# An adaLN transformer block on one core: score operands gathered by 16 transfers per half batch in place of 24, v by two per batch

## The reference

```python
x = L0_attn_x                              # 8 x 512 x 256, f32
mod = (silu(L0_c) @ L0_wmod).reshape(8, 6, 1, 256)
sa, ca, ga, sb, cb, gb = (mod[:, i] for i in range(6))   # gates ga, gb: |.| at least 0.25
h = layernorm(x) * (1 + ca) + sa
x = x + ga * attn_block(h)                 # LN, 16 heads of 16, band of 128 keys, softmax,
                                           # out-projection, LN, 256 -> 1024 -> 256 with gelu
h = layernorm(x) * (1 + cb) + sb
return x + gb * channel_mix(h)             # mixes each row with the one before; sigmoid(r) * (relu(k)^2 @ Wv)
```

## Time and profile before

| | |
|---|---|
| time, median of 3 runs | 644.75 us (642.35 to 646.23) |
| the profiled execution's own time | 644.62 us |
| its span, first to last instruction | 642.9 us |
| PE busy | 579.4 us (90%) |
| PE weight loads | 454.9 us (71%) |
| ACT busy | 449.8 us (70%) |
| DVE busy | 418.7 us (65%) |
| POOL busy | 384.1 us (60%) |
| transfers | 63516 packets, 55.74 MB, mean 87 GB/s |

### The profile page before, as it was taken

How to read it: one execution, slowest core, us unless ns; L and a number is a source line. 1 busy time by engine, 2 the same in 40 slices (tenths; PEclk the granted TensorE clock), 3 DMA queues, 4 the chain that set the end, 5 groups by cost and what they waited for, 6 DMA issues and landing times.

```text
span 642.9 us, 16628 instructions
## 1 busy us (share of the span) xinstructions
PE 579.4 (90%) x6494; PEld 454.9 (71%) x6494; DVE 418.7 (65%) x847; ACT 449.8 (70%) x758; POOL 384.1 (60%) x610
## 2 busy tenths in 40 slices
PE   5888888799889999989998999999899989999986
PEld 2667575669667777767766777677667768877775
DVE  4775584647676668667876868576857485365543
ACT  2533634588687978698869877887879788955542
POOL 3400874637775765857776767765777369835321
PEclk9978988799989999999999999999999999999999
DMA  7534321323441222433253414341333131311110
GB/s 239 194 92 128 84 58 52 86 68 102 112 115 53 79 57 69 124 91 104 57 136 83 112 44 112 108 114 47 94 97 95 51 97 44 93 36 34 34 42 33
DMA packets 63516, 55.74 MB, mean 87 GB/s; under 512 B 14459, under 2 KB 52669, under 8 KB 63438
## 3 DMA queue, kind: packets, MB, share of 16 engines
q1 hardware_dynamic: 60454, 52.64, 29.1%
q10 hardware_dynamic: 2984, 2.05, 1.2%
HBM read 22.31 MB, written 4.49 MB: 42 GB/s over the span
## 4 chain that ended last, share of the span: by engine, by line
PE 52%; DVE 16%; ACT 14%; SPq 5%; POOL 5%; issue 4%; DMA 3%; ACTq 0%; DVEq 0%; POOLq 0%
PE bank L351 4%; DVE nmax L1519 4%; PE bank L468 4%; PE quad L330 3%; PE bank L456 3%; PE bank L480 3%; PE bank L429 3%; PE bank L430 3%; PE bank L431 3%; PE quad L380 3%; PE bank L229 3%; ACT bank L1021 3%; SPq L2536 2%; SPq L2538 2%; PE quad L257 2%
## 5 line engine op out<-in xcount | busy, mean ns | idle before, releaser
L970 ACT ACTIVATE p<-quad,scale_s 128x768 f32<-128x768 f32 (+1 forms) x90 | 73.3, 825 | 17.4 <-PE quad L330 16.0
L2151 POOL TENSOR_SCALAR_AFFINE_SELECT p<-p 128x448 f32<-128x448 f32 x64 | 40.3, 630 | 73.9 <-ACT p L975 45.6
L1519 DVE TENSOR_REDUCE nmax<-quad 128x8 f32<-128x1032 f32 x64 | 78.9, 1233 | 2.2
L1021 ACT ACTIVATE bank<-bank,bias,scale_g 128x256 f32<-128x256 f32 x128 | 63.1, 532 | 17.3 <-PE bank L414 17.1
L412 PE MATMUL bank<-bt_hi,w_hi 128*128 128x256 f16 x256 | 70.3, 275 | 4.1 <-DVE hid_lo L1579 4.0
L429 PE MATMUL bank<-w_hi,hid_hi 128*128 128x256 f16 x256 | 69.9, 273 | 1.4 <-DVE hid_lo L1579 0.9
L413 PE MATMUL bank<-bt_lo,w_hi 128*128 128x256 f16 x256 | 69.9, 273 | 0.0
L414 PE MATMUL bank<-bt_hi,w_lo 128*128 128x256 f16 x256 | 69.8, 273 | 0.0
L431 PE MATMUL bank<-w_hi,hid_lo 128*128 128x256 f16 x256 | 69.8, 273 | 0.0
L430 PE MATMUL bank<-w_lo,hid_hi 128*128 128x256 f16 x256 | 69.8, 273 | 0.0
L2166 POOL TENSOR_TENSOR ps<-p 128x384 f32<-128x384 f32 x64 | 65.2, 1019 | 3.1 <-PE quad L363 1.3
(11 more groups left out here) (226 smaller groups left out, 1509.1 us busy)
## 6 DMA issues: line engine op xcount, KB each, us to landing
v_blk<-vn SPq DMA_DIRECT2D x64, 128.0 KB, 2.6
k_st<-kt_hi SPq DMA_DIRECT2D x120, 64.0 KB, 2.0
rb<-den_rows SPq DMA_DIRECT2D x16, 256.0 KB
x<-x SPq DMA_DIRECT2D x16, 256.0 KB, 3.1
out<-x SPq DMA_DIRECT2D x16, 256.0 KB, 2.3
q_st<-qt_hi SPq DMA_DIRECT2D x120, 32.0 KB, 1.9
k_st<-kt_lo SPq DMA_DIRECT2D x60, 64.0 KB, 2.0
xa<-x SPq DMA_DIRECT2D x7, 512.0 KB, 5.0
```

The source lines that it names most:

```text
L970: e.activation(p32[gp % SLOTS][:, c0:c0 + 2 * w].rearrange("p (n c) -> p n c", n=2), quad[:, b0:b0 + 2, 0:w], ACT.Exp, scale=scale_s[:, 1: ...
L1021: e.activation(dst, dst, ACT.Gelu_apprx_tanh, bias=bias_1[:, m:m + 1], scale=scale_g[:, 0:1]).then_inc(s_gl, 1)
L1519: e.tensor_reduce(nmax[:, :, :, qt].rearrange("p a j -> p j a"), quad[:, :, 2 * QB - 2:2 * WIN].rearrange("p j (c a) -> p j a c", a=2), AX ...
```

## The change

The high and low parts of q become two planes of one tile `q_two`, those of k two planes of `k_two`; the old names are views of them. One transfer then writes 64 rows of `q_st`, each row's high and low part after one another, and one writes 64 rows of `k_st` with each row of `kt_hi` twice. The third 32 rows are gathered as before. Four transfers per group take the place of six. `vn` and `v_blk` get another order of dimensions, so that two transfers of 512 KB, in pieces of 4 KB, move the v of a whole batch, where eight of 128 KB did. There is one `load_v(n)`, in the place of `load_v(n, 0)`; it waits for `s_av` of 2n, both contexts of the batch before. The rest of each engine's order is kept. The core of the diff:

```diff
-        qt_hi, qt_lo = sb("qt_hi", [P, L], F16), sb("qt_lo", [P, L], F16)
-        kt_hi, kt_lo = sb("kt_hi", [P, 2 * L], F16), sb("kt_lo", [P, 2 * L], F16)
+        q_two, k_two = sb("q_two", [P, 2, L], F16), sb("k_two", [P, 2, 2 * L], F16)
+        qt_hi, qt_lo, kt_hi, kt_lo = q_two[:, 0, :], q_two[:, 1, :], k_two[:, 0, :], k_two[:, 1, :]
...
-        vn = sb("vn", [P, NT, 2, 2, 2 * VW])
-        v_blk = sb("v_blk", [P, 2, 8, 2 * VW])
+        vn = sb("vn", [P, 2, NT, 2, 2 * VW])
+        v_blk = sb("v_blk", [P, 2, NT, 2, 2 * VW])
...
-                        e.wait_ge(s_stk[j], 6 * DMA * (u + 1))
+                        e.wait_ge(s_stk[j], 4 * DMA * (u + 1))
...
-                e.wait_ge(s_vin[half], 4 * DMA * (u // 2 + 1))
+                e.wait_ge(s_vin, 2 * DMA * (u // 2 + 1))
...
-                    for r, part in enumerate((qt_hi, qt_lo, qt_hi)):
-                        e.dma_start(q_st[2 * HD * r:2 * HD * (r + 1), half, j, :], part[src, :]).then_inc(s_stk[j], DMA)
-                    for r, part in enumerate((kt_hi, kt_hi, kt_lo)):
-                        e.dma_start(k_st[2 * HD * r:2 * HD * (r + 1), half, j, :], part[src, :]).then_inc(s_stk[j], DMA)
+                    e.dma_start(q_st[0:4 * HD, half, j, :], q_two[src, :, :]).then_inc(s_stk[j], DMA)
+                    e.dma_start(k_st[0:4 * HD, half, j, :], k_two[src, 0:1, :].broadcast_to([2 * HD, 2, 2 * L])).then_inc(s_stk[j], DMA)
+                    e.dma_start(q_st[4 * HD:SR, half, j, :], qt_hi[src, :]).then_inc(s_stk[j], DMA)
+                    e.dma_start(k_st[4 * HD:SR, half, j, :], kt_lo[src, :]).then_inc(s_stk[j], DMA)
...
-            def load_v(n, half):
+            def load_v(n):
...
                 e.wait_ge(s_v3, 4 * (n + 1))
-                hold(e, s_av, 2 * n - 1 + half if n else 0)
-                for a in range(2):
-                    for i in range(2):
-                        e.dma_start(v_blk[a:P:2, half, i:8:2, :], vn[KW * i:KW * (i + 1), :, a, half, :]).then_inc(s_vin[half], DMA)
+                hold(e, s_av, 2 * n)
+                for i in range(2):
+                    e.dma_start(v_blk[:, i, :, :, :], vn[KW * i:KW * (i + 1), :, :, :, :]).then_inc(s_vin, DMA)
...
             spread_den(0)
-            load_v(1, 0)
+            load_v(1)
             fold_den(1)
...
             save_den(2)
-            load_v(1, 1)
             spread_den(2)
             stacks(4, 0, 4)
             load_residual(0)
-            load_v(2, 0)
+            load_v(2)
             rows_gates()
...
             spread_den(3)
-            load_v(2, 1)
             load_mod_a(4)
```

More of the change, by code:

```diff
@@ L152, in adaln_block @@
         s_x, s_moda = sem("x_in"), sem("moda_in")
-        s_vin = [sem(f"v_in_{i}") for i in range(2)]
+        s_vin = sem("v_in")
         s_stk = [sem(f"stacks_{j}") for j in range(HQ)]
@@ L350, in context @@
                     for j in range(HQ):
-                        e.matmul(bank[32 * j:32 * j + 32, s * KW:s * KW + w], v_blk[:, half, s, 2 * j * HD:2 * (j + 1) * HD],
+                        e.matmul(bank[32 * j:32 * j + 32, s * KW:s * KW + w], v_blk[:, s % 2, s // 2, half, 2 * j * HD:2 * (j + 1) * HD],
                                  p32[(4 * u + j) % SLOTS][:, c:c + w], start=(s == 0), stop=(s == 7))
@@ L929, in high_qk @@
                 for j in range(HQ):
-                    hold(e, s_stk[j], 6 * DMA * u)
+                    hold(e, s_stk[j], 4 * DMA * u)
                 e.activation(qt_hi[:, :], ring_s.at["qk", u, 0][:, :], ACT.Identity, bias=bias_q[:, 2 * m:2 * m + 1]).then_inc(s_qh, 1)
@@ L943, in copy_v @@
                 e.wait_ge(s_v, 2 * n + t2 + 1)
-                hold(e, s_vin[0], 4 * DMA * n)
-                hold(e, s_vin[1], 4 * DMA * n)
-                rows = vn[:, 2 * t2:2 * t2 + 2, :, :, :].rearrange("p t a h (j b d) -> p t a (h j) b d", b=2, d=HD)
+                hold(e, s_vin, 2 * DMA * n)
+                rows = vn[:, :, 2 * t2:2 * t2 + 2, :, :].rearrange("p a t h (j b d) -> p a t (h j) b d", b=2, d=HD)
                 src = ring_s.at["v", n, t2][:, :].rearrange("p (t j b d) -> p t j b d", t=2, b=2, d=HD)
                 for a in range(2):
-                    e.activation(rows[:, :, a, :, a, :], src[:, :, :, a, :], ACT.Copy).then_inc(s_v3, 1)
+                    e.activation(rows[:, a, :, :, a, :], src[:, :, :, a, :], ACT.Copy).then_inc(s_v3, 1)
             def copy_den(u):
@@ L2645, in _ @@
             rows_bias()
-            load_v(0, 0)
-            load_v(0, 1)
+            load_v(0)
             stacks(1, 0, 2)
@@ L2693, in _ @@
                 store(u - 5)
-                load_v(b, 0)
+                load_v(b)
                 load_residual(u - 3)
-                load_v(b, 1)
                 fold_den(u)
@@ L2712, in _ @@
             store(7)
-            load_v(B - 2, 0)
+            load_v(B - 2)
             load_residual(9)
-            load_v(B - 2, 1)
             load_mod_o(4)
@@ L2725, in _ @@
             save_den(NU - 3)
-            load_v(B - 1, 0)
+            load_v(B - 1)
             spread_den(NU - 3)
@@ L2734, in _ @@
             load_mod_g(B - 2)
-            load_v(B - 1, 1)
             save_den(NU - 2)
```

## The result

The changed kernel took 656.88 us (median of 4 runs, 655.8 to 657.69) against 644.33 for the kernel before (median of 4, 642.35 to 646.23): a ratio of 1.0200, interval 1.0176 to 1.0224. It is slower, as forecast, by twice as much as forecast: 650.6 was predicted, with 654.6 as the upper end. The profiled execution took 655.8 us, span 654.1.

A forecast was written before the change was run, and what follows sets the result against it. PE was taken to bound the kernel (94% busy from 200 us), SP's 5% of the chain running beside it. Batch 1's +2.75 us, reduced to 2.25, grew to 6.0 with batch 2: 644.62 + 6.0 = 650.6 us, 8-in-10 range 645.8 to 654.6.

The forecast's parts named there:

- Gathers on SP: `stacks` gathers, 24 issues become 16 per half batch: 15.2 us become 10.1; 0 gained in the steady stage.
- Rival D: Larger transfers take proportionally longer to issue, 1.3 us more ahead of each `fold_den`: +2.6, 653.2 us; chance 0.04.
- Layouts, steady stage: Matmuls, ACT copies and weight loads keep counts and shapes: 0; from 200 us on PE is 94% full: 0.
- Gathers on ACT: Half batches 0 and 1, 12 issues become 8: 2.5 us less in ACT's queue, 0 gained.
- Batch 1: `load_v(1)` ahead of `fold_den(1)`: 1.05 MB takes 3.4 us, `rc` lands at 116.05 not 113.3, DVE and PE 2.75 late.
- What follows it: After batch 1, `stacks(4)` starts at 146.25 and lands by 160; ACT and PE waits go, shift falls to 2.25 us.
- Batch 2: `load_v(2)` ahead of `rows_gates`, `load_residual(1)` and `fold_den(3)`, which lands at 178.1; DVE and PE 6.0 us late in all.
- The sum: Whole kernel: profiled execution of 644.62 us plus 6.0 gives 650.6 us, 0.9% above.
- Rival A: At v's transfers, the small transfer passes the large ones, so only issue order costs: +2, 646.6 us; chance 0.15.
- Rival B: At `stacks(4)` and `high_qk(5)`, SP's chain gives time back if `rc(1)`, `rc(3)` are no later: 641.5 or 643 us; chance 0.13.
- Rival C: A 5 us stop at 174 may bring half-speed clock, 4 us losing 2, two stretches 3.5: 653 to 654 us; chance 0.10.

The follow-up runs named there:

- mv12: Changed kernel with `load_v(1)` moved behind `spread_den(1)` and `load_v(2)` behind `spread_den(3)`: 643.03 us, 0.9996 of the kernel before.
- two_q: Changed kernel with the second v transfer of batch 1 issued from ACT's queue, beside the first on SP: 657.26 us, ratio 1.0212 to before.
- stride: Changed kernel, each v transfer of batches 1 and 2 reading 64 source partitions two apart, not adjacent (wrong tokens): 650.50 us, ratio 1.0108 to before.
- small: Changed kernel, v transfers of batches 1 and 2 carrying a quarter of their bytes, same order and issues: 649.29 us, ratio 1.0071 to before.
- g_only: Kernel before with only the new gathers (16 transfers per half batch), v as before: 642.49 us, ratio 0.9972 to before.
- v_only: Changed kernel with the old gathers (24), so only v by two transfers is new: 656.02 us, ratio 1.0187 to before.

## Why the prediction was right in kind and wrong in size

*Gathers on SP:* right. 16 issues from 123.01 to 133.56, 10.55 us for the 10.1 forecast, at 0.57 to 0.61 each. Rival D fell with it: two issues of 512 KB took 1.24 us in front of `rc(1)`, no more than two of 128 KB. The 2.85 us of the two at 173.24 are not their size, as in `mv12` the same two took 1.25. One reading was off without changing the term: SP's wait for copied denominators, 96.0 us, is the largest of its waits but a third of their 280 us, not most. *Layouts, steady stage:* right, 0: from context 4 to the end 443.75 us for 443.6. *Gathers on ACT* lie ahead of context 1, where executions differ by more than they could cost: not shown.

*Batch 1:* right in mechanism, the size wrong, and this is the step that failed. The prediction gave 1.05 MB 3.4 us, at some 300 GB/s, and let `rc` land 0.45 us behind. In the slices of after, v's data run from 113.5 to about 118.5: 5.0 us, at 203 GB/s for the first half and faster after it. The rate was taken between the 128 KB transfers and `xa`, because the pieces were thought to matter; the source's partitions do, and by them the first were the nearest row. The bound of 4.4 us was too low as well: it took the engines for a fifth idle at 200 GB/s, and in `two_q` they were full at 203. Then `rc` is used at 120.47, 2 us behind the bulk of v and not 0.45. The slices show a thin tail after 118.5: small packets (under 512 B), `rc`'s for the most part, go out from 117.5 to 119.9 us, the last 18 of them from 119.7 on, right behind the last 4 KB packet of v. So `rc` landed when the latest DMA engine was through with v; why one was late no run tests. In `stride`, where the data stop short at 114.5, it is used at 115.03. Together PE's stop grew by 5.5 us, where 2.75 was forecast with 3.8 as the limit; the stretch grew by 4.65, mostly because PE was busy 0.75 us less in it (20.9 us for 21.6). That `rc` lies behind v, as the ring order has it, is plain: 6.6 us from its issue to its use, and 1.9 in `small`.

*What follows it:* right. `qt_hi` waits for `k_st` no more, and the stretch from context 2 to 3 is 0.85 us shorter; 0.5 was forecast. Either half of the change gives that alone: 29.9 us in `g_only` and in `v_only`.

*Batch 2:* the same error a second time. From the end of context 3 to `divide(3)` the prediction has 8.1 us (170.0 to 178.1), the trace 9.65 (173.13 to 182.78); before it was 4.35. `mod_rows` landed 6.9 us after that end and not 5.3: the rate again. So the stretch cost 5.6 in place of 3.75.

*The sum.* The spans differ by 11.2 us where 6.0 was forecast. Each place took 1.9 us more than its term, and the gain between them was 0.35 larger: 3.45 of the 5.2 us. 1.6 more lie ahead of context 1, where the two kernels differ in nothing that this account prices. The clock may be the cause: summed over windows of 2 us from 50 to 110, this execution had 16.2 us at the lower clock and that of before 13.6, and 2.6 us more at half speed would be some 1.3 us. That is not shown: `stride` had 17.1 us of it and context 1 at 110.06. By the medians the difference is 12.55.

*Rival A* (the small transfer passes) is out: `rc(1)` waited. *Rival B* has its condition met in `g_only` only: with `rc` left alone the gathers give about 0.3%, not told apart from nothing. *Rival C* (the clock) is true as a mechanism and not as a price of the change: after the second stop there is a low stretch that costs PE 1.65 us (28.05 us busy against 26.40 in `mv12`), but the kernel before has one there too, from 184 to 188, which costs it 2.1 (28.51 against 26.40). At the second place the two nearly cancel.

## What to carry to other kernels

A large transfer that nobody waits for yet is not free: look at which small transfer is issued behind it on the same queue, and who waits for that one; here two calls ahead of the denominators and the gate rows cost 12.5 us, and moving them behind gave all of it back (0.9996 of the time before). Take the rate of an on-chip transfer from a row whose source covers the same partitions, not from one with the same piece length. And when an experiment takes half of a stop away, read the idle time and the clock of that stretch, not the total alone: `small` got 3.5 us of its second stop back and lost 2.8 of them to slower matmuls.

## What was not expected of the hardware

A source on partitions 0 to 63 moved at 203 GB/s, one on 64 partitions spread over all 128 at 400. Of two transfers issued together on two queues, the second moved nothing for 2.5 us, until the first was through. With 1.05 MB queued SP's own issue is held: 1.85 us for `rc` behind v and 2.85 for the two of v at 173.24, where 0.63 and 1.24 are usual.

Executions of one kernel differ by up to 7 us, and their times go with the clock: of the ten of `g_only`, the four with a mean granted clock of 0.981 or more took 636.96 to 640.14 us, the six with 0.972 to 0.975 took 642.17 to 644.15. Part of it lies ahead of context 1. In the profiled execution of `g_only` (637.38) the window of 100 to 112 us is

```profile
100.00:112.00 12.00, 7.28 (x174) 5.81 (x171) 5.74 (x9) 7.52 (x17) 4.51 (x8) 1.00 0.22 51
```

with the clock at 1.00 and context 1 ending at 107.44; in `mv12` the clock is 0.85 there and the end at 111.44. What sets the clock in that stretch no run shows. A comparison of two single executions of this kernel is no better than that.
